# Decoder stack on one core: scores in two rounds of 32 rows, key copies half as wide, row transposes in another bank, two orders changed

## The chip, the cores and the metric

The kernel runs on one core of one Trainium2 chip. The metric is the device time in microseconds (us) of one execution; lower is better.

## The reference

Six attention phases over 32 batches of 64 tokens and width 128, with other work between them. All is float32.

```python
# one phase: q from x; k, v from x (phases 0, 2) or from ctx (1, 3, 4, 5)
Q, K, V = x @ wq + bq, src @ wk + bk, src @ wv + bv      # split into 16 heads of 8, in phase 5 8 heads of 16
A = softmax(where(mask == 0, a large negative, Q K^T / sqrt(dk)))   # phases 0 to 4 have a mask
x = x + (A V) @ wo                                       # then, by phase:
# 0, 1, 4: layer norm; after phase 1 also x = ln(x + relu(x w1 + b1) w2 + b2), then rms norm of it
# 2, 3: the next phase reads rms norm(x); after phase 3: top-2 of 8 experts and a shared one
# 5: x + w2 relu(w1 x + b1) + b2 is the output
```

## The kernel before, in words

A pair is two batches, 128 tokens; a phase has 16 pairs. The work of a pair is cut into stages, and every engine runs a loop over slots: in slot s it does the stage with offset `off` for pair s - off. The offsets are projection 0 (`OFF_PROJ`), values and mask 1 (`OFF_V`), scores 2 (`OFF_SCORE`), transposed probabilities and their product with the values 3 (`OFF_PV`), division by the row sums and output projection 4 (`OFF_OUT`), normalised rows turned to columns 5 (`OFF_XT`), and behind them feed-forward (6 to 9, pairs of phase 1), routing (6 to 9, pairs of phase 3) or the last layers (6 to 8, phase 5). Phases 0 to 3 run as one train of slots, 0 to 72; then come the expert blocks, which the change does not touch; then phases 4 and 5 as a second train. Some slots of a phase are written out, and some come from a hardware loop with addresses in registers. Each engine takes its instructions in the order of `slot`, so a wait holds up all that stands behind it on that engine. Buffers are doubled by the pair's parity.

**Scores.** To multiply all heads at once, GpSimd (POOL) writes `k_by_j`: the keys copied once for each head of a half, each copy with all but one head's rows set to zero by a column of `cst` (L494). TensorE (PE) then runs four products side by side, two halves of 64 rows of queries and keys into two banks, times two batches (L598). With 16 heads a half holds 8 heads, so a copy is 128x1024, and a product has 512 columns. The trace shows eight records, two for each float32 product. VectorE (DVE) takes the maxima `top` (L1140) and the differences `prob` (L1156), ScalarE (ACT) the exponentials (L986); PE transposes them in two halves (L631), ACT copies each half out (L915, L935), and PE multiplies (L759, L770).

**Rows.** The output projection L697 goes to `y`; DVE leaves `spread`, POOL takes the root with `pow` (`rstd` L502, `shift_n` L511), ACT writes `normed` (L922), PE transposes it in bank `B_PROJ` (`XT`, L672), and ACT copies it to `x_t` (L963). The rows of the feed-forward are transposed in bank `B_OUT` (`FB`, L662). Its own root is `rstd_f` (L444, POOL), read by `n_f` (L1118, DVE).

**Order of a slot on PE:** scores; feed-forward out (L616); both transposed halves; routing ranks (L644); values (L656); FB and XT transposes; queries and keys (L687, L688); output projection; feed-forward in (L708); router (L727); mask (L740); products with values (L759), a wait for all that the next scores need (`score_ready`), row sums (L770). **On POOL:** feed-forward, `scaled` and `x_tok` of stage 5, `k_by_j`, root of stage 4, routing. **On ACT:** L915, L922, feed-forward rows, L935, FB copy, queries and keys, XT copy, exponentials, values. **On DVE:** division (L1107, L1110), `n_f` and `y_f` of the feed-forward, `top`, mask, `prob`, routing (`picked` L1178 among it), `y` and its statistics.

## Time and profile before

| what | value |
|---|---|
| runs of the kernel | 704.16, 702.21, 697.53 us; median 702.21 |
| profiled execution | 700.95 us, its span 699.0 us |
| busy | PE 87%, DVE 76%, ACT 68%, POOL 59% |
| chain that ended last | PE 48%, issue 21%, DVE 14%, ACT 8%, POOL 7% |
| mean granted TensorE clock | 0.973 of full speed |

The span is from the first to the last instruction; 1.95 us of the profiled execution lie around it. Busy shares are means over stages with different limits. A timeline row has the start in us from the span's start, the duration, the engine, the line, the operation, what it writes and reads, and in brackets how long the engine was idle before it and what released it.

### The profile page before, as it was taken

What the parts mean: (1) busy time and instruction counts of PE and PEld (TensorE: products, weight loads), DVE (VectorE), ACT (ScalarE), POOL (GpSimd) and SP (SyncE); (2) the same over time, 40 slices, a digit from 0 to 9 for tenths busy, and PEclk for the clock granted to TensorE, in tenths of its full rate; (3) what the DMA queues carried; (4) which work ended last, traced back from release to release, by engine and by line L of the source; (5) the groups of instructions that cost most, each with busy time, mean ns of one, the idle gap of its engine ahead of it and who ended that gap; (6) DMA issues with size and microseconds to landing.
All of it is one profiled execution on the core that took longest, in us unless ns stands there. A gap on an engine that the chain in (4) does not pass through costs nothing.

```text
span 699.0 us, 24529 instructions
## 1 busy us (share of the span) xinstructions
PE 606.7 (87%) x8126; PEld 438.3 (63%) x8126; DVE 529.2 (76%) x1210; ACT 476.9 (68%) x1355; POOL 415.4 (59%) x641
## 2 busy tenths in 40 slices
PE   6888998989998989999767658899996878999996
PEld 3555656666666666666544434799994546666773
DVE  2988899777778899999999852344435788888894
ACT  3677788788878887878655534354533567788994
POOL 5676676778888765565566675055554466665220
PEclk9999999999999999999999978999999899999997
DMA  6433433222444401010111001122225000100110
GB/s 199 122 93 90 105 84 84 53 66 56 107 125 114 126 25 31 26 31 26 32 32 32 25 29 36 35 61 69 66 62 135 17 25 24 30 12 22 36 31 27
DMA packets 49817, 41.97 MB, mean 60 GB/s; under 512 B 6569, under 2 KB 44333, under 8 KB 48704
## 3 DMA queue, kind: packets, MB, share of 16 engines
q1 hardware_dynamic: 41472, 23.13, 11.9%
q10 hardware_dynamic: 5984, 13.45, 8.1%
q0 software_dynamic: 2272, 4.24, 1.8%
q8 instruction: 52, 0.85, 0.5%
q14 instruction: 37, 0.30, 0.1%
HBM read 25.41 MB, written 14.79 MB: 57 GB/s over the span
## 4 chain that ended last, share of the span: by engine, by line
PE 48%; issue 21%; DVE 14%; ACT 8%; POOL 7%; DMA 1%; DVEq 0%; ACTq 0%; POOLq 0%; SPq 0%
PE ps L598 6%; PE ps L824 5%; PE ps L835 5%; PE ps L631 4%; PE ps L759 3%; DVE inv L1107 3%; ACT normed L922 3%; PE ps L687 3%; PE ps L790 3%; PE ps L770 2%; PE ps L708 2%; PE ps L616 2%; DVE prob L1156 2%; PE ps L688 2%; DVE picked L1178 2%
## 5 line engine op out<-in xcount | busy, mean ns | idle before, releaser
L494 POOL TENSOR_TENSOR k_by_j<-k_t,cst 128x1024 f32<-128x1024 f32 (+1 forms) x96 | 168.8, 1758 | 102.8 <-ACT k_t L952 63.0
L1140 DVE TENSOR_REDUCE top<-ps 128x16 f32<-128x1024 f32 (+1 forms) x96 | 108.3, 1128 | 16.6 <-PE ps L598 16.4
L631 PEld LDWEIGHTS ps<-cst,prob 128*128 128x128 f32 x704 | 78.5, 143 | 57.4 <-ACT prob L986 41.1
L986 ACT ACTIVATE prob<-prob 128x1024 f32<-128x1024 f32 (+1 forms) x96 | 95.2, 992 | 20.4 <-DVE prob L1156 19.8
L1156 DVE TENSOR_TENSOR prob<-ps,top 128x1024 f32<-128x1024 f32 (+1 forms) x96 | 108.3, 1128 | 0.7
L1107 DVE RECIPROCAL inv<-ps 128x128 f32<-128x128 f32 x96 | 91.5, 953 | 22.0 <-PE ps L770 21.2
L598 PE MATMUL ps<-k_by_j,q_t 64*64 64x512 f32 (+1 forms) x768 | 102.3, 604 | 0.5 <-POOL k_by_j L494 0.4
L631 PE MATMUL ps<-cst,prob 128*128 128x128 f32 x704 | 98.4, 282 | 1.2 <-ACT prob L986 1.2
L1000 ACT ACTIVATE v<-ps 64x64 f32<-64x64 f32 x320 | 69.0, 216 | 14.2 <-PE ps L770 11.3
L915 ACT ACTIVATE prob_t<-ps 128x512 f32<-128x512 f32 (+1 forms) x96 | 53.8, 560 | 36.2 <-PE ps L631 35.5
L540 POOL DMA_INDIRECT expert_out<-rows_out,rows_in x39 | 38.3, 982 | 53.8 <-DVE rows_out L1309 27.0
L759 PE MATMUL ps<-prob_t,v 128*32 128x64 f32 x2816 | 60.5, 225 | 0.5 <-ACT prob_t L935 0.5
L502 POOL TENSOR_TENSOR rstd<-spread,half_neg 128x1 f32<-128x1 f32 x80 | 44.7, 559 | 24.6 <-DVE spread L1238 22.3
L770 PE MATMUL ps<-prob_t,cst 128*32 128x128 f32 x1408 | 58.2, 278 | 0.8 <-issue 0.8
L759 PEld LDWEIGHTS ps<-prob_t,v 128*32 128x32 f32 x2816 | 44.8, 111 | 20.4 <-issue 18.3
L935 ACT ACTIVATE prob_t<-ps 128x512 f32<-128x512 f32 (+1 forms) x96 | 53.0, 552 | 0.0
L687 PE MATMUL ps<-x_t,wat 128*128 128x128 f32 (+1 forms) x192 | 42.9, 306 | 6.7 <-DMA stage_kv<-in_x_t 5.9
L478 POOL TENSOR_TENSOR scaled<-normed,rows 128x128 f32<-128x128 f32 x48 | 22.0, 459 | 33.4 <-ACT normed L922 33.4
L656 PE MATMUL ps<-wat,stage_kv 128*128 128x128 f32 x192 | 40.3, 292 | 1.7 <-ACT k_t L950 1.3
L824 PE MATMUL ps<-rows_t,first_w 128*128 128x128 f32 x312 | 41.3, 275 | 0.0
L697 PE MATMUL ps<-wat,heads_t 128*128 128x128 f32 x192 | 38.6, 283 | 3.1 <-DVE heads_t L1110 2.7
L835 PE MATMUL ps<-mow,hid_t 128*128 x312 | 41.2, 275 | 0.0
(159 smaller groups left out, 1267.3 us busy)
## 6 DMA issues: line engine op xcount, KB each, us to landing
sorted_rows<-zero_rows ACTq DMA_DIRECT2D x32, 276.2 KB, 2.7
stage_m<-in_m SPq DMA_DIRECT2D x80, 64.0 KB
mow<-in_mow SPq DMA_DIRECT2D x18, 256.0 KB, 3.0
stage_kv<-in_ctx_t SPq DMA_DIRECT2D x64, 64.0 KB
rows_in<-sorted_rows SPq DMA_DIRECT2D x39, 65.0 KB
x_t<-in_x_t SPq DMA_DIRECT2D x16, 64.0 KB, 1.9
stage_kv<-in_x_t SPq DMA_DIRECT2D x16, 64.0 KB
stage_kv<-x_t SPq DMA_DIRECT2D x16, 64.0 KB
```

Of the source, the lines that this page charges most:

```text
L494: pool.tensor_tensor(k_by_j[:, p, 0:nj, :], k_t[:, p:p + 1, :].broadcast_to([128, nj, TOK]), cst[:, cj:cj + nj].unsqueeze(2).broadcast_to( ...
L598: mm = pe.matmul(ps[S * b:S * b + S, 2 * p + bank, 0:nj * S].rearrange("p (h k) -> p h k", k=S), q_t[rows_h, p, S * b:S * b + S], k_by_j[r ...
L631: mm = pe.transpose(ps[:, 2 * p + half, k * 128:(k + 1) * 128], prob[:, p, q * 128:(q + 1) * 128], ident)
L759: mm = pe.matmul(ps[32 * g:32 * g + 32, B_HEADS, S * b:S * b + S], vb[:, p, b, q, :], prob_t[:, p, half, c * 128 + S * b:c * 128 + S * b + S],
L770: mm = pe.matmul(ps[32 * g:32 * g + 32, B_HEADS, 128:128 + TOK], own_ones(pr, k), prob_t[:, p, half, c * 128:c * 128 + TOK], start=k == 0, ...
L824: mm = pe.matmul(ps[:, B_H[j % 2], c * 128:(c + 1) * 128], first_w[:, j % 2, c * 128:(c + 1) * 128], rows_t[:, j % 2, :], start=True, stop ...
L835: mm = pe.matmul(ps[:, B_Y[j % 2], 0:D], hid_t[:, j % 2, c * 128:(c + 1) * 128], mow2[:, bass.ds(e, 1), c * 128:(c + 1) * 128].rearrange(" ...
L986: act.activation(prob[:, p, 0:w], prob[:, p, 0:w], ACT.Exp, scale=float(D // heads(pr)) ** -0.5).then_inc(exp_d, 1)
L1000: ins = act.activation(dst, src[:, :, par, :].rearrange("r (g k) d -> r g k d", k=2), ACT.Copy)
L1107: dve.reciprocal(inv[:, p, :], ps[:, B_HEADS, 128:128 + TOK]).then_inc(inv_d, 1)
L1140: dve.tensor_reduce(top[:, p, 0:nh].rearrange("p (b h) -> p b h", b=2), sc, AX.X, ALU.max).then_inc(top_d, 1)
L1156: dve.tensor_tensor(prob[:, p, 0:nh * S].rearrange("p (b h k) -> p b h k", b=2, k=S), sc, top[:, p, 0:nh].rearrange("p (b h) -> p b h", b= ...
```

## The change

1. `k_by_j` has one copy for each head of a group of 32 rows: four copies (two with 8 heads) in place of eight (four). The scores are made in two rounds: round 0 takes groups 0 and 2, round 1 groups 1 and 3, each round four products of half as many columns as before. Round 1 stands between the two transposed halves of the pair ahead, and waits for round 0 through `round_d`.
2. XT and FB transposes are written to free columns of bank `B_HEADS` and stand behind the query and key projections. They wait for `heads_d`; the products with values, which write that bank, wait for the copies `xt_e` and `f_xt`.
3. The wait `score_ready` in the midst of the products with values goes; its waits stand ahead of round 0.
4. On ACT L922 stands ahead of L915, and the FB copy behind the query and key copies. On POOL the root of stage 4 stands ahead of `k_by_j`.

```diff
         q_t, k_t = sb("q_t", [128, 2, TOK]), sb("k_t", [128, 2, TOK])
-        k_by_j = sb("k_by_j", [128, 2, 8, TOK])
+        k_by_j = sb("k_by_j", [128, 2, 4, TOK])
...
         B_PROJ, B_HEADS, B_OUT, B_F = 4, 5, 6, 7
-        FB, OUT, XT = (slice(128 * n, 128 * n + 128) for n in range(1, 4))
+        OUT, XT, FB = (slice(128 * n, 128 * n + 128) for n in range(1, 4))
...
 
-                pr = at(OFF_PROJ)
-                if pr is not None:
-                    p, nj = pr.p, heads(pr) // 2
-                    cj = C_J16 if nj == 8 else C_J8
-                    wait_pair(pool, k_e, pr)
-                    wait_pair(pool, score_d, pr, 2)
-                    pool.tensor_tensor(k_by_j[:, p, 0:nj, :], k_t[:, p:p + 1, :].broadcast_to([128, nj, TOK]),
-                                       cst[:, cj:cj + nj].unsqueeze(2).broadcast_to([128, nj, TOK]), ALU.mult)\
-                        .then_inc(kj_d, 1)
                 pr = at(OFF_OUT)
                 if pr is not None and POST[pr.phase] != "none":
                     p = pr.p
@@ -511,6 +503,15 @@
                         pool.tensor_tensor(shift_n[:, p, :], minus[:, p, :], rstd[:, p, :], ALU.mult).then_inc(shift_d, 1)
                     else:
                         pool.sem_inc(shift_d, 1)
+                pr = at(OFF_PROJ)
+                if pr is not None:
+                    p, nj = pr.p, heads(pr) // 4
+                    cj = C_J16 if nj == 4 else C_J8
+                    wait_pair(pool, k_e, pr)
+                    wait_pair(pool, score_d, pr, 2)
+                    pool.tensor_tensor(k_by_j[:, p, 0:nj, :], k_t[:, p:p + 1, :].broadcast_to([128, nj, TOK]),
+                                       cst[:, cj:cj + nj].unsqueeze(2).broadcast_to([128, nj, TOK]), ALU.mult)\
+                        .then_inc(kj_d, 1)
...
-
-            def score(pr):
-
-                p, nj = pr.p, heads(pr) // 2
+            def score_round(pr, r):
+
+                if r == 1:
+                    wait_pair(pe, round_d, pr)
+                p, nj = pr.p, heads(pr) // 4
                 masked = MASKED[pr.phase]
                 for bank in range(2):
-                    rows_h = slice(S * bank, S * bank + S)
+                    rows_g = slice(32 * (2 * bank + r), 32 * (2 * bank + r) + 32)
                     for b in range(2):
                         mm = pe.matmul(
-                            ps[S * b:S * b + S, 2 * p + bank, 0:nj * S].rearrange("p (h k) -> p h k", k=S),
-                            q_t[rows_h, p, S * b:S * b + S], k_by_j[rows_h, p, 0:nj, S * b:S * b + S],
-                            start=not masked, stop=True, skip_group_check=True)
-                mm.then_inc(score_d, 1)
+                            ps[S * b:S * b + S, 2 * p + bank, r * nj * S:(r + 1) * nj * S].rearrange("p (h k) -> p h k", k=S),
+                            q_t[rows_g, p, S * b:S * b + S], k_by_j[rows_g, p, 0:nj, S * b:S * b + S],
+                            start=not masked and r == 0, stop=True, skip_group_check=True)
+                return mm
...
                 pr = at(OFF_SCORE)
                 if pr is not None:
-                    if isinstance(pr.n, int):
-                        score_ready(pr)
-                    score(pr)
+                    p = pr.p
+                    wait_pair(pe, pt1_e, pr, 2)
+                    if MASKED[pr.phase]:
+                        wait_pair(pe, mask_d, pr)
+                    wait_pair(pe, q_e, pr)
+                    wait_pair(pe, kj_d, pr)
+                    score_round(pr, 0).then_inc(round_d, 1)
...
@@ -631,6 +630,9 @@
                             mm = pe.transpose(ps[:, 2 * p + half, k * 128:(k + 1) * 128],
                                               prob[:, p, q * 128:(q + 1) * 128], ident)
                         mm.then_inc(done, 1)
+                        scored = at(OFF_SCORE)
+                        if half == 0 and scored is not None:
+                            score_round(scored, 1).then_inc(score_d, 1)
...
                     wait_pair(pe, v_e, pr, 1)
-                    turned = at(OFF_XT + 1)
-                    if turned is not None:
-                        wait_pair(pe, xt_e, turned)
                     mm = pe.matmul(ps[:, B_PROJ, 256:384], stage_kv[:, p, :], wat[:, ph, 2, :], start=True, stop=True)
                     mm.then_inc(vproj_d, 1)
...
-                    pe.transpose(ps[:, B_OUT, FB], xn_f[:, done.p, :], ident).then_inc(f_back, 1)
-                pr = at(OFF_XT)
-                if pr is not None:
-                    wait_pair(pe, norm_d, pr)
-                    projected = at(OFF_PROJ + 1)
-                    if projected is not None:
-                        wait_pair(pe, k_e, projected)
-                    valued = at(OFF_V + 1)
-                    if valued is not None:
-                        wait_pair(pe, v_e, valued)
-                    pe.transpose(ps[:, B_PROJ, XT], row_buffer(pr), ident).then_inc(xt_d, 1)
...
                         .then_inc(proj_d, 1)
+                pr = at(OFF_SCORE)
+                if pr is not None and at(OFF_PV) is None:
+                    score_round(pr, 1).then_inc(score_d, 1)
+
+                divided = at(OFF_OUT)
+                pr = follows(at, OFF_FB, FF)
+                if pr is not None:
+                    if divided is not None:
+                        wait_pair(pe, heads_d, divided)
+                    wait_own(pe, f_xn, pr)
+                    pe.transpose(ps[:, B_HEADS, FB], xn_f[:, pr.p, :], ident).then_inc(f_back, 1)
+                pr = at(OFF_XT)
+                if pr is not None:
+                    if divided is not None:
+                        wait_pair(pe, heads_d, divided)
+                    wait_pair(pe, norm_d, pr)
+                    pe.transpose(ps[:, B_HEADS, XT], row_buffer(pr), ident).then_inc(xt_d, 1)
+
                 pr = at(OFF_OUT)
                 if pr is not None:
...
                     wait_pair(pe, heads_d, pr)
-                    before = follows(at, OFF_FB, FF)
-                    if before is not None:
-                        wait_own(pe, f_xt, before)
-
...
                     wait_pair(pe, v_e, pr)
                     wait_pair(pe, heads_d, pr, 1)
+                    turned = at(OFF_XT)
+                    if turned is not None:
+                        wait_pair(pe, xt_e, turned)
+                    turned = follows(at, OFF_FB, FF)
+                    if turned is not None:
+                        wait_own(pe, f_xt, turned)
                     wait_pair(pe, pt0_e, pr)
...
 
-                    following = at(OFF_V)
-                    if following is not None:
-                        score_ready(following)
...
                         .then_inc(l_o, 1)
-                pr = at(OFF_PV)
-                if pr is not None:
-                    p = pr.p
-                    w = 128 * (heads(pr) // 4)
-                    wait_pair(act, pv_d, pr, 2)
-                    wait_pair(act, pt0_d, pr)
-                    act.activation(prob_t[:, p, 0, 0:w], ps[:, 2 * p, 0:w], ACT.Copy).then_inc(pt0_e, 1)
                 pr = at(OFF_XT)
                 if pr is not None and POST[pr.phase] == "ln":
                     p = pr.p
@@ -921,6 +915,13 @@
                     wait_pair(act, res_d, pr, 2)
                     act.activation(normed[:, p, :], y[:, p, :], ACT.Identity, bias=shift_n[:, p, :], scale=rstd[:, p, :])\
                         .then_inc(norm_d, 1)
+                pr = at(OFF_PV)
+                if pr is not None:
+                    p = pr.p
+                    w = 128 * (heads(pr) // 4)
+                    wait_pair(act, pv_d, pr, 2)
+                    wait_pair(act, pt0_d, pr)
+                    act.activation(prob_t[:, p, 0, 0:w], ps[:, 2 * p, 0:w], ACT.Copy).then_inc(pt0_e, 1)
...
 
-                pr = follows(at, OFF_FB, FF)
-                if pr is not None:
-                    wait_own(act, f_back, pr)
-                    act.activation(x_t[:, bass.ds(pr.i * TOK, TOK)], ps[:, B_OUT, FB], ACT.Copy, scale=v("n1"))\
-                        .then_inc(f_xt, 1)
...
                             act.activation(dst[:, p, :], src, ACT.Copy).then_inc(done, 1)
+
+                pr = follows(at, OFF_FB, FF)
+                if pr is not None:
+                    wait_own(act, f_back, pr)
+                    turned = at(OFF_XT)
+                    if turned is not None:
+                        wait_pair(act, xt_d, turned)
+                    act.activation(x_t[:, bass.ds(pr.i * TOK, TOK)], ps[:, B_HEADS, FB], ACT.Copy, scale=v("n1"))\
+                        .then_inc(f_xt, 1)
                 pr = at(OFF_XT)
                 if pr is not None:
                     ph = pr.phase
                     wait_pair(act, xt_d, pr)
-                    dst, src = x_t[:, bass.ds(pr.i * TOK, TOK)], ps[:, B_PROJ, XT]
+                    dst, src = x_t[:, bass.ds(pr.i * TOK, TOK)], ps[:, B_HEADS, XT]
```

The columns of `cst` are made to fit: `C_J16` is `r % 32 // 8 == arange(4)`, and `C_J8` is `r % 32 // 16 == arange(2)`.

## Rows read from the trace of the kernel before

**Rows 1.** Timeline of PE, phase 1: start, us, engine, line, op [idle before]
```profile
108.19 1.09 PE L598 MATMUL ps<-k_by_j,q_t 64*64 64x512 f32 x8
...
109.21 1.09 PE L631 MATMUL ps<-cst,prob 128*128 128x128 f32 x8
...
110.14 0.39 PE L656 MATMUL ps<-wat,stage_kv 128*128 128x128 f32 x2
...
110.99 0.33 PE L672 MATMUL ps<-cst,normed 128*128 128x128 f32 x1 [0.47 <-ACT normed L922]
...
111.16 0.40 PE L687 MATMUL ps<-x_t,wat 128*128 128x128 f32 x2
...
111.39 0.39 PE L688 MATMUL ps<-stage_kv,wat 128*128 128x128 f32 x2
...
112.27 0.65 PE L759 MATMUL ps<-prob_t,v 128*32 128x64 f32 x32
...
113.29 1.09 PE L598 MATMUL ps<-k_by_j,q_t 64*64 64x512 f32 x8
```

**Rows 2.** Timeline of ACT in the same slot
```profile
111.81 0.37 ACT L950 ACTIVATE q_t<-ps,vec 128x128 f32<-128x128 f32 x1 [0.39 <-PE ps L688]
...
112.33 0.46 ACT L963 ACTIVATE x_t<-ps,vec 128x128 f32<-128x128 f32 x1
```

**Rows 3.** Timeline of PE, phase 0, first slots
```profile
37.77 0.33 PE L672 MATMUL ps<-cst,normed 128*128 128x128 f32 x1 [1.46 <-ACT normed L922]
```

**Rows 4.** Timeline of DVE and ACT, phase 2 without feed-forward
```profile
286.10 1.21 DVE L1140 TENSOR_REDUCE top<-ps 128x16 f32<-128x1024 f32 x1
...
287.37 1.22 DVE L1156 TENSOR_TENSOR prob<-ps,top 128x1024 f32<-128x1024 f32 x1
...
288.62 1.06 ACT L986 ACTIVATE prob<-prob 128x1024 f32<-128x1024 f32 x1 [0.75 <-DVE prob L1156]
```

**Rows 5.** Timeline of POOL, DVE and PE, slot with feed-forward
```profile
206.71 0.55 POOL L502 TENSOR_TENSOR rstd<-spread,half_neg 128x1 f32<-128x1 f32 x1
...
207.63 0.55 POOL L444 TENSOR_TENSOR rstd_f<-spread_f,half_neg 128x1 f32<-128x1 f32 x1
...
208.23 0.34 DVE L1118 TENSOR_SCALAR n_f<-y_f,mom_f,rstd_f 128x128 f32<-128x128 f32 x1
...
209.03 0.29 DVE L1126 TENSOR_TENSOR y_f<-ps,x_tok 128x128 f32<-128x128 f32 x1 [0.47 <-PE ps L616]
...
210.85 0.33 PE L662 MATMUL ps<-cst,xn_f 128*128 128x128 f32 x1 [0.76 <-ACT xn_f L929]
...
213.60 0.15 DVE L1235 TENSOR_SCALAR spread<-moments 128x1 f32<-128x1 f32 x1
```

**Rows 6.** Line L1107, one per slot: count, ns least/median/most, first and last start
```profile
L1107 DVE RECIPROCAL inv<-ps x6: 956/957/959, 199.4 to 236.8; 128x128 f32<-128x128 f32 x6
...
L1107 DVE RECIPROCAL inv<-ps x12: 945/947/948, 265.1 to 318.4; 128x128 f32<-128x128 f32 x12
...
L1107 DVE RECIPROCAL inv<-ps x11: 947/952/957, 318.4 to 390.3; 128x128 f32<-128x128 f32 x11
```

**Rows 7.** Timeline of DVE and POOL in one routing slot
```profile
370.62 2.54 DVE L1178 TENSOR_TENSOR picked<-hot,rank 128x16 f32<-128x16 f32 x1
...
371.21 1.90 POOL L494 TENSOR_TENSOR k_by_j<-k_t,cst 128x1024 f32<-128x1024 f32 x1
```

**Rows 8.** Source lines of DVE without a PSUM operand, whole kernel: count, ns least/median/most
```profile
L1178 DVE TENSOR_TENSOR picked<-hot,rank x16: 157/166/2544, 334.2 to 427.5; 128x16 f32<-128x16 f32 x16
...
L1238 DVE CUSTOM_DVE_ANT_0 squares<-y x32: 291/824/1729, 228.1 to 411.3; 128x128 f32<-128x128 f32 x32
...
L1320 DVE TENSOR_TENSOR x_tok<-mow,x_tok x8: 415/762/1681, 530.4 to 567.9; 128x256 f32<-128x256 f32 x8
```

**Rows 9.** Timeline of POOL and PE in phase 5, eight heads
```profile
667.08 1.04 POOL L494 TENSOR_TENSOR k_by_j<-k_t,cst 128x512 f32<-128x512 f32 x1 [2.70 <-ACT k_t L952]
...
667.32 0.66 PE L598 MATMUL ps<-k_by_j,q_t 64*64 64x256 f32 x8
```

More of the change, by code:

```diff
@@ L70 @@
 BIASED = {0: 0, 1: 1, 4: 2}
-C_ID, C_J16, C_J8, C_IOTA, C_BASE = 0, 128, 136, 140, 148
-C_STEP, C_UPTO, C_BLOCK = 156, 172, 236
+C_ID, C_J16, C_J8, C_IOTA, C_BASE = 0, 128, 132, 134, 142
+C_STEP, C_UPTO, C_BLOCK = 150, 166, 230
 C_O16 = C_BLOCK + JB
@@ L266, in build @@
         neg_d, mask_d = sem("neg_d"), sem("mask_d")
+        round_d = sem("round_d")
         minus_d, shift_d = sem("minus_d"), sem("shift_d")
@@ L581, in _ @@
             pe.wait_ge(loaded["wat"], 16)
-            def score_ready(pr):
-                wait_pair(pe, pt1_e, pr, 2)
-                if MASKED[pr.phase]:
-                    wait_pair(pe, mask_d, pr)
-                wait_pair(pe, q_e, pr)
-                wait_pair(pe, kj_d, pr)
-            def score(pr):
-                p, nj = pr.p, heads(pr) // 2
+            def score_round(pr, r):
+                if r == 1:
+                    wait_pair(pe, round_d, pr)
+                p, nj = pr.p, heads(pr) // 4
                 masked = MASKED[pr.phase]
                 for bank in range(2):
-                    rows_h = slice(S * bank, S * bank + S)
+                    rows_g = slice(32 * (2 * bank + r), 32 * (2 * bank + r) + 32)
                     for b in range(2):
                         mm = pe.matmul(
-                            ps[S * b:S * b + S, 2 * p + bank, 0:nj * S].rearrange("p (h k) -> p h k", k=S),
-                            q_t[rows_h, p, S * b:S * b + S], k_by_j[rows_h, p, 0:nj, S * b:S * b + S],
-                            start=not masked, stop=True, skip_group_check=True)
-                mm.then_inc(score_d, 1)
+                            ps[S * b:S * b + S, 2 * p + bank, r * nj * S:(r + 1) * nj * S].rearrange("p (h k) -> p h k", k=S),
+                            q_t[rows_g, p, S * b:S * b + S], k_by_j[rows_g, p, 0:nj, S * b:S * b + S],
+                            start=not masked and r == 0, stop=True, skip_group_check=True)
+                return mm
             def slot(at):
@@ L652, in slot @@
                     wait_pair(pe, v_e, pr, 1)
-                    turned = at(OFF_XT + 1)
-                    if turned is not None:
-                        wait_pair(pe, xt_e, turned)
                     mm = pe.matmul(ps[:, B_PROJ, 256:384], stage_kv[:, p, :], wat[:, ph, 2, :], start=True, stop=True)
                     mm.then_inc(vproj_d, 1)
-                done = follows(at, OFF_FB, FF)
-                if done is not None:
-                    wait_own(pe, f_xn, done)
-                    pe.transpose(ps[:, B_OUT, FB], xn_f[:, done.p, :], ident).then_inc(f_back, 1)
-                pr = at(OFF_XT)
-                if pr is not None:
-                    wait_pair(pe, norm_d, pr)
-                    projected = at(OFF_PROJ + 1)
-                    if projected is not None:
-                        wait_pair(pe, k_e, projected)
-                    valued = at(OFF_V + 1)
-                    if valued is not None:
-                        wait_pair(pe, v_e, valued)
-                    pe.transpose(ps[:, B_PROJ, XT], row_buffer(pr), ident).then_inc(xt_d, 1)
                 pr = at(OFF_PROJ)
@@ L1349, in constants @@
     cst[:, C_ID:C_ID + 128] = np.eye(128)
-    cst[:, C_J16:C_J16 + 8] = r[:, None] % S // 8 == np.arange(8)
-    cst[:, C_J8:C_J8 + 4] = r[:, None] % S // 16 == np.arange(4)
+    cst[:, C_J16:C_J16 + 4] = r[:, None] % 32 // 8 == np.arange(4)
+    cst[:, C_J8:C_J8 + 2] = r[:, None] % 32 // 16 == np.arange(2)
     cst[:, C_IOTA:C_IOTA + E] = np.arange(E)
```

## Prediction

> **What bounds the kernel now.** I read the page's shares first (in the table above): PE is busy 87% and DVE 76%, and no engine is full on average. So I went through the timeline stage by stage and asked in each which loop from one slot to the next has no slack. There are four kinds of slot.
>
> *Layer-norm slots without other work* (phases 0, 1 and 4, some 30 of them). PE goes from scores to scores in 5.10 us and stands 0.47 ahead of the XT transpose for `normed` [rows 1]. The loop is XT, queries and keys, their copy on ACT, the `k_by_j` copy of 1.90 on POOL (the length is that of [rows 7]), the root queued behind it, `normed`, XT again [rows 1, 2]. In the first slots of phase 0 that wait is 1.46 [rows 3].
>
> *Feed-forward slots* (14 full ones). The period is (236.8 - 199.4) / 5 = 7.5 [rows 6], PE waits 0.76 for `xn_f` [rows 5], and DVE is in step with POOL: `n_f` starts 0.05 after `rstd_f` ends, at 208.18 [rows 5].
>
> *Routing slots.* Ten periods take 390.3 - 318.4 = 71.9 us [rows 6]. `picked`, 16 elements in a row, takes 0.16 at least and 0.17 in the median, but here 2.54: it ends at 373.16, when the `k_by_j` copy of POOL ends (373.11) [rows 7, 8]. Where all of DVE's operands lie in SBUF, it waits for a copy of POOL to end. `squares` takes 0.29 at least and 0.82 in the median for this reason, and the combination of expert rows (L1320) 0.42 at least and 1.68 at most [rows 8]. The Trainium skill says the same in "SBUF — State Buffer", in the section on the shared pair: it is an exclusive lock for the whole instruction, taken by a DVE operation with two SBUF inputs or a GpSimd operation, and the loser blocks. The trace agrees (2.54 against 0.16).
>
> *Phase 5* has copies of 1.04 and scores of 0.66 [rows 9], and PE without idle time.
>
> **The change, part by part.**
>
> *Rounds.* The score records span 1.09 with 512 columns and 0.66 with 256 [rows 1, 9], so 256 columns are worth 0.43. The step from scores to the next instruction is 109.21 - 108.19 = 1.02; with 256 columns it is 0.59, and 0.16 of each is fixed. Two rounds cost 1.18, 0.16 more for each slot with 16 heads, and the same for 8 heads. A group of 32 rows is not in the trace. Below, a round can cost nothing fixed, 0.43; above, two of the four products of a round might not overlap, and it takes 1.02 like the whole set of before. I take 0.59, the nearest row. The maxima now wait for round 1 and so for half of the transposes: 0.59 + 0.465 + 0.66 = 1.72 after the start of the scores, where it was 1.09 (half of the transposes is (110.14 - 109.21) / 2 = 0.465) [rows 1].
> That rounds interleaved with full transposes change the array's tiling twice more per slot is what the Trainium skill warns of in "TensorEngine Tiling (Array Packing)", Key Properties: a change of tiling mode drains TensorE. By the rule each entry costs something; the fixed 0.16 of a set of four may be this drain.
>
> *Narrow copies.* A 128x512 copy took 1.04 [rows 9] against 1.90: 0.86 less of POOL for each of 80 slots. In phase 5 it is 128x256 and not in the trace; by the same step it is 1.04 - 0.43 = 0.6, at best 0.52, at worst 1.04.
>
> *The root ahead of the copy, `normed` first.* The loop through the copy is broken in the layer-norm slots. What is late next? PE's own order, with the new wait for `xt_e` ahead of the products with values. The key projection starts at 0.59 + 0.465 + 0.59 + 0.465 + 0.23 + 0.23 = 2.57 after the scores (steps of 0.23 between projections, 111.39 - 111.16 [rows 1]). From there ACT's copy of the queries starts 0.42 later, the XT copy 0.52 after that, and it lasts 0.46 [rows 1, 2]: 3.97. The products start at 4.0 and the next scores 113.29 - 112.27 = 1.02 later: 5.02 to 5.05. Before, the products followed 0.88 after the key projection [rows 1]; now it is 1.43, so about 0.4 of PE's old wait comes back at the new place. Behind that wait are queued the products, the row sums and the next scores, and DVE's division waits for them. A second loop comes with round 1, since it stands behind transposes that wait for the exponentials: 0.465 + 0.66 for transposes and round 1, 1.27 from maxima to differences, 1.25 to the exponentials, 1.06 for them [rows 4], and two hand-overs of 0.05: 4.8. So a layer-norm slot takes 5.05 for 5.10, with up to 0.2 more where the hardware loop ran slower: -2 over 30 slots (-5 to +2).
> *Plain slots of phase 2.* DVE loses its block at `squares`, but the period before is (318.4 - 265.1) / 11 = 4.85 [rows 6], and the new loop of 4.8 takes over: 0 (-3 to +3).
> *Start.* The wait of 1.46 in the first slots goes down to the steady one, and the first scores wait for a copy that is 0.86 shorter: -3 (0 to -4).
>
> *Feed-forward slots.* Here the new order on POOL closes a loop. The copy now stands behind the root of stage 4, which waits for `spread`, and ahead of `rstd_f`, for which DVE stands at `n_f`. From the end of `spread`: 0.1 to the root, 207.63 - 206.71 = 0.92 to the end of `shift_n`, 1.0 for the copy [rows 9], 0.55 for `rstd_f`, 0.05 to `n_f`; `n_f` 0.34; and 213.75 - 209.03 = 4.72 from `y_f` to the end of `spread` [rows 5]. The sum is 7.7, and the period before is 7.5. The earlier feed-forward transposes and the gone wait of 0.76 on PE bring nothing then: 0 over 14 slots. Bounds: if a few of DVE's steps shorten with POOL less busy, or PE alone sets it (7.5 - 0.76 + 0.16 = 6.9), -8; if the loop costs its full sum, +3.
>
> *Routing slots.* The copy now runs behind the root, while DVE divides and takes maxima out of PSUM, and 4 us ahead of `picked`. The period of full slots, about 7.8 (with two short slots of 5.5 the other eight make up 71.9 with 7.6 on average), loses 2.54 - 0.16 = 2.38 and gets the later maxima (1.72 - 1.09 = 0.63): 6.05. Two slots at 5.0 and eight at 6.05 are 58.4, so -13.5. `chosen` waits behind the copy, 1.0 later after the root, but PE reaches the ranks then only. What can keep part of the block: POOL's indirect transfers and its two copies of rows can still meet `picked`. The gain has 5 and 13.5 as bounds; I take 10.
>
> *Restart of phase 4.* Four of the combinations took 1.1 to 1.7 where 0.42 is enough, 4.3 in sum (least and most of eight are in the row) [rows 8]. They run just behind `spread`, now ahead of the copy. First copy -0.9; the transposes and the second round ahead of the maxima give back 0.6 in four slots: -3 (0 to -5).
>
> *Phase 5.* PE is full, and gets 0.16 for the second round and part of the new wait, since ACT's copies need 1.1 to 1.4 after the keys: +0.2 in 16 slots, +3 (0 to +6). No block on DVE's last sum is worth anything while PE is the bound.
>
> *No cost:* the moved `score_ready` (its waits are long over by the next slot, as the copy is made two slots ahead), the bank change itself (`heads_d` is awaited by the output projection right behind).
>
> Sum: -3 - 2 + 0 + 0 - 10 - 3 + 3 = -15. Against the profiled 700.95 this is 686; the median of the runs lies 1.3 above it, and I predict 687.5 beside a median of 702.2.
>
> **The rivals.**
>
> *A. Rounds that do not overlap (slower).* If a round of 32 rows takes not 0.59 but 0.59 + d, then some 30 layer-norm, 13 plain, 8 routing and 16 slots of phase 5 get 2d, or d by the second loop: about 65 x 2d = 130d. It eats the 15 from d = 0.12. With d = 0.2, half way to products that run by twos, it is +26: 713. For it: no product of 32 rows is in the trace, and each entry into another tiling drains. Against: four products of 64 rows overlap, and 32 products on tiles of 32 columns start within 0.47. The drain rule of the page, with the fixed 0.16 twice per round in place of once, is d = 0.16: 708.
>
> *B. The block moves instead of going (same).* POOL's row copies and transfers come back to back, and `picked` waits for their end; the copy meets `n_f` and the mask row instead. Routing then gives 4, the restart 1.5, and feed-forward slots lose 0.1 each: 698. For it: POOL is busy 59% of the span. Against: the median of `picked` is 0.17 with those transfers running.
>
> *C. Feed-forward slots go with PE (faster still).* If `n_f` does not bind, 14 slots go to 6.9 at best: -8, and 679. Against: the sum of 7.7 above, for which every step is in the rows.
>
> **How the numbers follow.** Forecast 55%, C 15%, B 17%, A 13%. The half widths of the terms together (root of the sum of squares of 5, 5, 3, 3, 3, 2) are about 9 either way; the range from 677 to 704 holds the forecast, C and B, and leaves most of A and the ends out. A difference of under 1% (7 us) is about what a measurement of this kernel can tell from none. Faster by more than that, under 695.2: forecast and C, some of B: 0.72. Within 1%: most of B, the edges of forecast and A: 0.17. Slower: A: 0.11.
>
> **What would show it.** `k_by_j` at 1.04 in 80 slots. Score records 0.6 to 0.7 in span, two sets per slot; a longer set is A. `picked` at 0.2 and L1107 at 6.0 to 6.5 apart between 340 and 390; if it stays at 7, B. In layer-norm slots PE idle ahead of L759 with ACT's XT copy (L963) as releaser, and none ahead of L672. In feed-forward slots `n_f` waiting on `rstd_f`, and the period still 7.4 to 7.7; at 7.0, C. Phase 5 at 3.8 or more. The prediction is wrong above all if one loop that I found closed has slack, since 14 or 30 slots hang on each.

## The result and the profile after

The changed kernel takes 705.25 us (median of 16 runs, 702.43 to 708.17) beside 702.17 for the kernel before on the same chip (697.53 to 704.76, 16 runs): a ratio of 1.0055, interval 1.0034 to 1.0076. The forecast was 687.5. The profiled execution took 707.85 with a span of 706.0, 7.0 more than before. The page's first part of the changed kernel (busy us, share, instructions):

```profile
PE 617.7 (87%) x8894; PEld 455.4 (64%) x8894; DVE 496.1 (70%) x1210; ACT 496.3 (70%) x1355; POOL 337.4 (48%) x641
```

POOL is busy 78 us less and DVE 33 less, and the kernel is not faster: the work that went was not what the slots wait for.

`inv` (L1111 now) runs once per slot, so its starts divide the span. The table is worked out from these starts; "changed again" is a second profile of the changed kernel, "before again" one of the kernel before. The last column is the prediction's term.

```
stage (slots)          before  before again  changed  changed again  difference  predicted
start (4)               40.4      37.1        42.6       43.1          +2.2       -3
phase 0 (9)             47.4      47.5        48.9       48.9          +1.4 }
phase 1 (6)             30.7      30.7        32.1       32.1          +1.4 }     -2
phase 4, full (10)      51.7      51.7        53.6       53.6          +2.0 }
feed-forward (20)      141.5     141.6       138.4      138.4          -3.2        0
plain (12)              58.4      58.4        61.4       61.4          +3.0        0
routing (10)            71.9      71.5        61.1       61.0         -10.8      -10
drain and experts      157.5     156.3       165.6      159.3          +8.0      none
restart (4)             27.9      27.9        25.8       26.4          -2.1       -3
phase 5 (17)            60.9      61.0        66.1       66.1          +5.2       +3
```

The difference column compares the first profiles. In the slots from phase 0 to routing, and in phases 4 and 5, two profiles of one program agree within 0.4 us. The start and the experts do not repeat: the experts took 137.8 to 145.9 us over all the profiles of this study, and changed and changed again differ by 6.3 in drain and experts. The view by windows shows a part of why. The first fence is of the changed kernel, the second of the same kernel profiled again (columns: window, PE busy with its instructions, granted clock, DMA share, GB/s), each from the last slot of the drain on.

```profile
404.70:424.70 20.00, 13.13 (x38) 0.62 0.10 31
...
444.70:464.70 20.00, 20.00 (x171) 0.94 0.20 53
```

```profile
402.40:422.40 20.00, 12.84 (x45) 0.74 0.10 31
...
442.40:462.40 20.00, 19.94 (x179) 1.00 0.22 58
```

PE, busy only 13 of 20 us there, was granted 0.62 instead of 0.74 of its clock, and 0.94 for 1.00 in the next but one window; the experts alone are 3.6 us longer there. So most of the +8.0 belongs to that execution. Without drain and experts the differences sum to -0.9; with those of changed again (+1.8) to +0.9, and the medians say +3.1. The 2 us between are of the size by which start and experts differ between executions, and were not resolved further. The forecast had -15 in the place of the -0.9, so its terms are off by 14 in sum.

The layer-norm slot that answers to [rows 1], PE and then ACT in the timeline of the changed kernel:

```profile
107.33 0.66 PE L593 MATMUL ps<-k_by_j,q_t 32*64 32x256 f32 x8
107.92 0.66 PE L630 MATMUL ps<-cst,prob 128*128 128x128 f32 x4
108.51 0.66 PE L593 MATMUL ps<-k_by_j,q_t 32*64 32x256 f32 x8
109.10 0.66 PE L630 MATMUL ps<-cst,prob 128*128 128x128 f32 x4
109.59 0.39 PE L655 MATMUL ps<-wat,stage_kv 128*128 128x128 f32 x2
...
110.04 0.39 PE L672 MATMUL ps<-stage_kv,wat 128*128 128x128 f32 x2
110.26 0.27 PE L690 MATMUL ps<-cst,normed 128*128 128x128 f32 x1
...
111.65 0.65 PE L763 MATMUL ps<-prob_t,v 128*32 128x64 f32 x32 [0.55 <-issue]
...
112.67 0.66 PE L593 MATMUL ps<-k_by_j,q_t 32*64 32x256 f32 x8
```

```profile
110.47 0.37 ACT L946 ACTIVATE q_t<-ps,vec 128x128 f32<-128x128 f32 x1
...
110.98 0.46 ACT L968 ACTIVATE x_t<-ps,vec 128x128 f32<-128x128 f32 x1
```

Three things are to be seen. The round of 32 rows takes what was forecast (span 0.66, step 0.59). The wait at XT is gone: L690 follows L672 without idle time, where it was 0.47 [rows 1]. And the whole of it is back, 0.55 long, ahead of the products with values (L763), which start 0.21 after ACT's XT copy ends (110.98 + 0.46 = 111.44). The profile names "issue" as releaser and not ACT. But in nearly every layer-norm slot, plain slot and slot of phase 5 the products start 0.20 to 0.21 after that copy ends, with idle times ahead of them of mostly 0.54 to 0.62, 0.27 to 0.35 and 0.30 to 0.38; and the profile of run 2 names the copy. The chain that ended last holds, in this stretch of the changed kernel, nothing but PE and this piece (start, length, what):

```profile
110.76 0.34 PE ps L738 x4
111.10 0.55 issue
111.65 0.65 PE ps L763 x32
112.30 0.44 PE ps L771 x16
```

The source lines that answer to [rows 8] and [rows 6] (count, ns least/median/most, first and last start; the first `inv` row is eleven periods of full feed-forward slots, the second the plain slots, the third the routing slots):

```profile
L1182 DVE TENSOR_TENSOR picked<-hot,rank x16: 157/164/247, 338.4 to 424.8; 128x16 f32<-128x16 f32 x16
...
L1242 DVE CUSTOM_DVE_ANT_0 squares<-y x32: 291/292/293, 231.9 to 408.6; 128x128 f32<-128x128 f32 x32
...
L1324 DVE TENSOR_TENSOR x_tok<-mow,x_tok x8: 409/424/425, 527.3 to 568.9; 128x256 f32<-128x256 f32 x8
...
L1111 DVE RECIPROCAL inv<-ps x12: 956/957/958, 157.9 to 238.9; 128x128 f32<-128x128 f32 x12
...
L1111 DVE RECIPROCAL inv<-ps x13: 956/957/958, 261.9 to 323.3; 128x128 f32<-128x128 f32 x13
...
L1111 DVE RECIPROCAL inv<-ps x11: 950/952/958, 323.3 to 384.4; 128x128 f32<-128x128 f32 x11
```

Every block of DVE is gone: `picked` at most 0.25 (2.54 before), `squares` 0.29 throughout, the combination 0.43 at most. Routing slots are 6.11 apart on average; the full ones are 6.3 apart (7.8 before), where 6.05 was forecast. Plain slots are (323.3 - 261.9) / 12 = 5.12 apart, where 4.86 was to stay.

A feed-forward slot, DVE and POOL in the timeline of the changed kernel, answering to [rows 5]:

```profile
210.30 0.15 DVE L1239 TENSOR_SCALAR spread<-moments 128x1 f32<-128x1 f32 x1
...
213.03 0.35 DVE L1122 TENSOR_SCALAR n_f<-y_f,mom_f,rstd_f 128x128 f32<-128x128 f32 x1 [1.30 <-POOL rstd_f L445]
```

```profile
211.45 1.04 POOL L512 TENSOR_TENSOR k_by_j<-k_t,cst 128x512 f32<-128x512 f32 x1
212.45 0.55 POOL L445 TENSOR_TENSOR rstd_f<-spread_f,half_neg 128x1 f32<-128x1 f32 x1
```

DVE stands 1.30 for `rstd_f` behind root and copy, as forecast; the period is (238.9 - 157.9) / 11 = 7.36 (7.56 over the same eleven slots before, 7.7 as the sum had it).

### The profile page after: what moved, and what is told of

Its sections match the earlier page's. It is cut to its first block, busy times and chain, and to the rows that moved or that the text cites. A ratio compares the mean times of both kernels' runs of the same rounds, so it can differ in the third digit from the quotient of the medians.

```text
span 706.0 us, 25942 instructions
## 1 busy us (share of the span) xinstructions
PE 617.7 (87%) x8894; PEld 455.4 (64%) x8894; DVE 496.1 (70%) x1210; ACT 496.3 (70%) x1355; POOL 337.4 (48%) x641
## 4 chain that ended last, share of the span: by engine, by line
PE 64%; issue 17%; DVE 8%; POOL 6%; ACT 2%; DMA 1%; DVEq 0%; POOLq 0%; SPq 0%; ACTq 0%
PE ps L593 12%; PE ps L630 10%; PE ps L763 6%; PE ps L825 5%; PE ps L836 5%; PE ps L771 4%; PE ps L738 3%; PE ps L791 3%; PE ps L671 2%; PE ps L655 2%; PE ps L672 2%; PE ps L695 2%; PE ps L801 2%; DVE prob L1160 2%; POOL rstd_f L445 1%
## 5 line engine op out<-in xcount | busy, mean ns | idle before, releaser
L593 PE MATMUL ps<-k_by_j,q_t 32*64 32x256 f32 (+1 forms) x1536 | 124.3, 393 | 1.2 <-issue 0.3
L512 POOL TENSOR_TENSOR k_by_j<-k_t,cst 128x512 f32<-128x512 f32 (+1 forms) x96 | 93.1, 970 | 66.6 <-ACT k_t L948 37.4
L630 PE MATMUL ps<-cst,prob 128*128 128x128 f32 x704 | 119.5, 290 | 2.3 <-ACT prob L990 2.1
L630 PEld LDWEIGHTS ps<-cst,prob 128*128 128x128 f32 x704 | 76.5, 143 | 62.1 <-issue 47.1
L1111 DVE RECIPROCAL inv<-ps 128x128 f32<-128x128 f32 x96 | 91.8, 956 | 22.8 <-PE ps L771 20.0
L763 PE MATMUL ps<-prob_t,v 128*32 128x64 f32 x2816 | 60.5, 225 | 30.5 <-issue 27.7
L763 PEld LDWEIGHTS ps<-prob_t,v 128*32 128x32 f32 x2816 | 46.7, 111 | 53.1 <-issue 53.1
L936 ACT ACTIVATE prob_t<-ps 128x512 f32<-128x512 f32 (+1 forms) x96 | 53.6, 558 | 19.0 <-PE ps L630 18.3
L593 PEld LDWEIGHTS ps<-k_by_j,q_t 32*64 32x64 f32 x1536 | 40.8, 133 | 38.0 <-issue 37.4
L541 POOL DMA_INDIRECT expert_out<-rows_out,rows_in x39 | 38.3, 983 | 53.3 <-DVE rows_out L1313 29.3
L771 PE MATMUL ps<-prob_t,cst 128*32 128x128 f32 x1408 | 60.0, 277 | 0.0
L671 PE MATMUL ps<-x_t,wat 128*128 128x128 f32 (+1 forms) x192 | 39.5, 289 | 7.8 <-DMA stage_kv<-in_x_t 7.3
L825 PE MATMUL ps<-rows_t,first_w 128*128 128x128 f32 x312 | 42.9, 282 | 0.0
L825 PEld LDWEIGHTS ps<-rows_t,first_w 128*128 128x128 f32 x312 | 39.4, 198 | 0.0
```

Of the source, the lines that this page charges most:

```text
L512: pool.tensor_tensor(k_by_j[:, p, 0:nj, :], k_t[:, p:p + 1, :].broadcast_to([128, nj, TOK]), cst[:, cj:cj + nj].unsqueeze(2).broadcast_to( ...
L593: mm = pe.matmul(ps[S * b:S * b + S, 2 * p + bank, r * nj * S:(r + 1) * nj * S].rearrange("p (h k) -> p h k", k=S), q_t[rows_g, p, S * b:S ...
L630: mm = pe.transpose(ps[:, 2 * p + half, k * 128:(k + 1) * 128], prob[:, p, q * 128:(q + 1) * 128], ident)
L763: mm = pe.matmul(ps[32 * g:32 * g + 32, B_HEADS, S * b:S * b + S], vb[:, p, b, q, :], prob_t[:, p, half, c * 128 + S * b:c * 128 + S * b + S],
L771: mm = pe.matmul(ps[32 * g:32 * g + 32, B_HEADS, 128:128 + TOK], own_ones(pr, k), prob_t[:, p, half, c * 128:c * 128 + TOK], start=k == 0, ...
L825: mm = pe.matmul(ps[:, B_H[j % 2], c * 128:(c + 1) * 128], first_w[:, j % 2, c * 128:(c + 1) * 128], rows_t[:, j % 2, :], start=True, stop ...
```

## The experiments

The suspects are the two rounds, the new XT place with its wait ahead of the products, the order on POOL, and the start. In the edits only the core stands. Runs 1 to 4, 5 to 8, and 9 and 10 shared a chip each; the kernel before had medians of 699.04, 699.43 and 701.11 there. All ratios are to the kernel before on the same chip; runs of different groups are compared by their ratios. Runs 3, 5 and 6 have four executions each, 8 and 9 one, the others ten. A run's stage times come from one profiled execution, which can lie some us off the median. Feed-forward periods are over the eleven slots of the first section.

**1. The rounds alone.**

```
 before.py: score(pr)  ->  score_round(pr, 0) ... score_round(pr, 1), k_by_j 4 copies wide;
 POOL, ACT and the transposes as in the kernel before
```

> The kernel before with the two rounds and the narrow copies alone; transposes, orders of ACT and POOL and the early wait for the scores stay as before. Theory W (the changed kernel loses its gain to the new wait of the products with values for the XT copy): without that wait layer-norm slots are set by PE's own work at about 4.9, plain slots of phase 2 at 4.9, phase 5 at 3.8; the routing slots keep a block of a narrow copy, 7.8 - 0.9 = 6.9; feed-forward slots 7.2. Sum about 688. Rival R (the rounds themselves cost more than the narrow copies give, 0.3 per slot for four changes of tiling): 96 slots by 0.3 less the narrow copies' 10, about 720; layer-norm slots stay at 5.3.

Measured: 692.84, ratio 0.9911 (0.9874 to 0.9947). Plain slots 4.94 apart, routing 6.59, phases 0, 1 and 4 128.2 in all (129.7 before, 134.6 changed), phase 5 60.6. The rounds with narrow copies don't lose in the layer-norm slots or in phase 5; in the plain slots they lose 1.0 in all. Their largest gain lies in the feed-forward stage, 134.4 for 141.5 before, where the changed kernel has 138.4, and so has run 3, which differs from this one in little but the orders on POOL and ACT. In routing `picked` still runs into the copy, for the shorter time that it has now:

```profile
L1187 DVE TENSOR_TENSOR picked<-hot,rank x16: 159/171/1682, 326.7 to 414.7; 128x16 f32<-128x16 f32 x16
```

**2. The change without rounds**, one set of 64 rows with copies of 1.90.

```
 after.py: score_round(pr, 0/1)  ->  score(pr), k_by_j 8 copies wide,
 score_ready(following) between the products as before
```

> The changed kernel with the scores in one set of 64 rows and the wide copies again (the wait for the next scores stands in the midst of the products as before); transposes in the bank of heads and both new orders stay. Theory W: layer-norm slots still wait for the XT copy: key projection at 2.4, then 1.6 and 1.0: 5.0. Feed-forward slots get 0.9 longer through the wide copy ahead of rstd_f, 8.2; routing slots 7.0; phase 5 3.7. Sum about 705. Rival R: slots shrink by the full cost of the rounds, sum under 695.

Measured: 696.73, ratio 0.9952 (0.9932 to 0.9971). Phase 4 is 50.7 (53.6 changed), plain slots 4.79, phase 5 63.0 (66.1 changed), but feed-forward slots went from 7.36 to 8.20: the copy of 1.90 in the loop of root, copy and `rstd_f`. The sum of 705 was missed by 8, above all since routing slots did not go to 7.0: they take 62.1 in all with the wide copy too (61.1 changed, 71.9 before), and `picked` is 0.25 at most. Here the profile names ACT's XT copy ahead of the products with values, in the slot that answers to [rows 1]:

```profile
113.76 0.65 PE L759 MATMUL ps<-prob_t,v 128*32 128x64 f32 x32 [0.52 <-ACT x_t L967]
```

**3. XT and feed-forward transposes back** in their old banks and places, all else as changed.

```
 after.py, PE: transpose(ps[:, B_HEADS, XT]) behind the projections
   -> transpose(ps[:, B_PROJ, XT]) ahead of them;
 no wait for xt_e ahead of the products with values
```

> The changed kernel with the XT and FB transposes in their old banks and places, with their old waits; rounds, narrow copies, and both new orders stay. Theory W: PE has no wait ahead of the products, and none at XT since normed comes first: layer-norm slots 4.9 (now 5.34), plain 4.85 (now 5.1), phase 5 3.75 (now 4.0), feed-forward slots unchanged at 7.35 (set by rstd_f behind the copy), routing unchanged at 6.3. Sum about 688. Rival R: layer-norm slots stay above 5.2 and the time within 1% of the changed kernel.

Measured: 692.29, ratio 0.9888 (0.9856 to 0.9919). Phases 0, 1 and 4 take 127.8 (5.0 to 5.2 for a slot, not 4.9), phase 5 60.4, plain slots 4.94, routing unchanged at 61.0. In nine of the plain slots PE stands at the first transposes for the exponentials, the second loop of the prediction:

```profile
272.75 0.66 PE L630 MATMUL ps<-cst,prob 128*128 128x128 f32 x4 [0.16 <-ACT prob L988]
```

So the new transposes, with the wait that comes with them, cost 1.7% or 12 us (the stages from phase 0 to phase 5 without drain and experts give 14), and the order on POOL is worth its routing gain without them.

**4. The copy ahead of the root again.**

```
 after.py, POOL: k_by_j ahead of rstd, minus, shift_n instead of behind them
```

> The changed kernel with the key copy ahead of the root on POOL again, all else as changed. Theory P (in feed-forward slots DVE waits at n_f for rstd_f behind the copy; in routing slots the late copy is what frees picked): feed-forward slots go to 7.0 from 7.35, routing slots to 6.9 from 6.3, layer-norm slots unchanged at 5.34 since their bound is the XT copy. Sum 704 to 706. Rival: the order on POOL is worth what it was meant for in the layer-norm slots, and these lengthen to over 5.5: 712.

Measured: 701.88, ratio 1.0036 (1.0011 to 1.0061). Feed-forward slots fell from 7.36 to 6.68, routing slots rose from 6.11 to 6.55 (`picked` at most 1.68 again); phases 0, 1 and 4 stayed at 134.7. Root or copy first is indifferent to the layer-norm slots as long as XT's copy bounds them, and the two other kinds give -10.6 (feed-forward, the shorter slots at both ends included) and +4.4. The profiles bear this out (spans 699.2 and 706.0, drain and experts 166 in both), the ratios show only 1.3 of it. Part of that is which execution was profiled: the changed kernel's lies 2.6 above its median, this one's 0.9 below. The rest is open.

**5. Copies deferred in feed-forward slots** (on top of 3): there POOL makes the copy one slot later, behind `rrms_f`.

```
+    pr = at(OFF_V)        # behind rrms_f
+    if pr is not None and follows(at, OFF_FN, FF) is not None: k_by_j copy
-    if pr is not None:    # behind shift_n
+    if pr is not None and follows(at, OFF_FN - 1, FF) is None: k_by_j copy
```

> The kernel with the transposes back in their old banks and places (692.3 us, 0.989 of before), and the key copy of feed-forward slots made in the next slot, behind rstd_f and rrms_f; elsewhere it stays behind the root. If n_f behind the copy is what sets the 11 full feed-forward slots (7.44 there, 6.68 with the copy first), they go to 6.7, the ramps before and behind with them: -9 in the span, routing unchanged at 6.1. About 683. Rival: something else holds these slots, and only the copy ahead of the root frees them: 7.4 and no change.

Measured: 686.84, ratio 0.9853 (0.9803 to 0.9903), an interval that overlaps that of run 3. Feed-forward slots 7.17 (7.44 in run 3, 6.7 expected), `n_f` without a wait; routing stays 60.8. The wait was there and went, but half of the gain did not come: PE is now without a marked idle time, and from the values to the output projection it takes 1.20 with the transposes in their old place, where the kernel of run 4 takes 0.89. So in these slots the new place looks the better one; no run changes it alone.

**6. The same with one set of 64 rows and wide copies.**

```
 run 5: score_round(pr, 0/1)  ->  score(pr), k_by_j 8 copies wide
```

> The last kernel, but with the scores in one set of 64 rows and the wide copies, as before the change. Theory: two rounds are a loss wherever PE's order is the bound, and their narrow copies buy nothing once the copy stands behind the root and out of the way of rstd_f. Layer-norm slots 4.7 (DVE's own work) for 5.0 to 5.2, plain slots 4.8, feed-forward slots 6.6 to 6.8, routing 6.3, phase 5 3.4 to 3.5: 672 to 678. Rival: the wide copy of 1.9 is missed somewhere else, in routing slots (7.0) or in feed-forward slots (7.5): 690.

Measured: 676.96, ratio 0.9684 (0.9630 to 0.9738), the fastest of all, 22 us under the kernel before. Of the change it keeps the root ahead of the copy and `normed` first on ACT, and it has the deferred copies of run 5; the wait `score_ready` is back too. The plain slots, and `picked`, in the source lines of this kernel:

```profile
L1117 DVE RECIPROCAL inv<-ps x13: 956/958/959, 254.8 to 308.3; 128x128 f32<-128x128 f32 x13
```

```profile
L1188 DVE TENSOR_TENSOR picked<-hot,rank x16: 158/165/254, 322.6 to 407.2; 128x16 f32<-128x16 f32 x16
```

Plain slots are (308.3 - 254.8) / 12 = 4.46 against 4.94 in run 5, and the restart 23.4 against 26.9; routing gives 2.0 back (62.9) and the feed-forward stage 3.1 (136.7 for 133.7, where 6.6 to 6.8 for a slot was expected and 7.2 measured). Phases 4 and 5 are unchanged to 0.1, so there the rounds cost nothing; 4.7 and 3.4 were expected and 5.05 and 3.55 measured. The total fell in the range by other terms than those forecast. With the copies off the path, the rounds are a net cost of 10 us by the medians (686.84 against 676.96, four executions each) and of 7 by the profiled spans (681.8 and 674.6): 5.8 in plain slots, 3.5 in the restart and 1.7 in the start, less what feed-forward and routing give back; 2.2 more lie in drain and experts.

**7. The changed kernel with ACT's XT copy ahead of the copies of queries and keys.**

```
 after.py, ACT: x_t<-ps (XT) ahead of q_t, k_t <- ps
```

> The changed kernel with one order changed on ACT: the XT copy ahead of the copies of queries and keys. Theory W: the products wait for this copy, which ends 1.40 after the key projection starts; alone in front it ends about 0.9 to 1.0 after, so layer-norm slots go from 5.34 to 4.9, plain ones from 5.12 to 4.9, phase 5 from 3.8 to 3.5, feed-forward unchanged at 7.36. About 693. Rival R (the rounds on PE set these slots): no change from 705.

Measured: 695.9, ratio 0.9947 (0.9918 to 0.9976). Moving one copy of 0.46 by two places on ACT gives back 1.1%. The idle time ahead of the products fell from 0.55 to 0.23 in the timeline of this kernel, and phase 4 to 50.6, the value without the new transposes:

```profile
113.14 0.65 PE L763 MATMUL ps<-prob_t,v 128*32 128x64 f32 x32 [0.23 <-issue]
```

So the wait for XT's copy is what run 3 took away. Plain slots are 4.99. Phase 5 keeps over half of its loss (63.9, or 3.8 for a slot, where 3.5 was expected).

**8. The changed kernel again**, one execution.

> The changed kernel once more, for a second profile. If the 5.5 us that the expert blocks took more in its first profile come from the clock of TensorE in that one execution, they move; if they belong to the kernel, 145 stays, where before had 140.

Measured: 702.17, span 700.4. All slot stages repeated, drain and experts came 6.3 shorter (first section).

**9. The kernel before again**, one execution.

> The kernel before once more, one look, for the spread between two profiles of one program. The drain behind routing took 17.8 us, the experts 139.8 and the first score round's stage 24.5 in its first profile; TensorE's granted clock in the drain differed between executions of the changed kernel (20.3 and 17.6 us). If that is the program's, this profile repeats 139.8 and 17.8 within 0.3; if it is chance, the experts come anywhere from 139.8 to 142 here, and the loops of the other stages repeat within 0.3%.

Measured: 696.33, span 694.4. The experts repeated (140.0), the drain came 1.4 shorter, and the start 3.3 shorter; the other stages repeated within 0.1 but for routing, 0.4 shorter. In the start PE's records have two lengths: in its first profile the 128x128 pair of the key projection took 0.63 until 14 us and 0.39 from 20 on, here 0.39 from 12.6 on, after an idle time of 0.74. These are lengths as of the two levels of the clock, 1.2 and 2.4 GHz, though the granted clock reads 1.00 throughout. When PE comes to the higher level differs between executions, and the start that is 3.3 shorter goes with it.

**10. Round 1 at once in the slots without products.**

```
 after.py, PE:  score_round(pr, 0)
+               if at(OFF_PV) is None: score_round(pr, 1)    # was behind the projections
```

> The changed kernel, but in the slots that have no products with values yet round 1 of the scores stands right behind round 0, not behind the values and the projections of the next pair. Theory (the start loses its 2.7 us because round 1 of the first pair, ready at 10.5, waits for projections whose input lands at 13.9, until 14.6): the first maxima start at 11.2 to 11.7 us of the span rather than 15.8, the stage up to the second reciprocal takes 24.5 to 25 us for 27.3, the restart of phase 4 perhaps 1 less than 25.8, and all else stays: 702 to 703 beside 705.2. Rival (the load of the third pair sets the start in any case): maxima early, stage still 27, time unchanged.

Measured: 701.17, ratio 1.0012 (0.9974 to 1.0049), against 1.0055 for the changed kernel: 3 us less, though the intervals overlap. The profiled execution, 694.99, is the fastest of the ten and 6 under their median, so its stage times flatter the kernel. The first maxima on DVE, in this kernel and then in the changed one:

```profile
11.62 1.22 DVE L1143 TENSOR_REDUCE top<-ps 128x16 f32<-128x1024 f32 x1 [5.18 <-PE ps L593]
```

```profile
15.76 1.22 DVE L1144 TENSOR_REDUCE top<-ps 128x16 f32<-128x1024 f32 x1 [9.62 <-PE ps L593]
```

The stage to the first `inv` is 22.7 for 27.3. Part of that is again PE's records reaching 0.39 earlier (from 18.6 us, beyond 23.4 in the changed kernel). That this goes with the placement shows over all profiles: in the seven of kernels that hold round 1 back, the first projection at the short length comes at 23.9 to 29.3 us, in the five others (both of the kernel before, runs 2, 6 and 10) at 11.2 to 19.7. No run separates it from the later maxima. The restart stayed at 26.3, so the placement of round 1 is not what holds it at 26 to 27.

## Why the prediction was wrong

*Bounds and blocks: right.* DVE's blocks, the loop of root, copy and `rstd_f`, and PE's wait for XT were where they were said to be. Routing gave 10.8 for 10, the restart 2.1 for 3; the narrow copies take 1.04, and 0.61 in phase 5 for the 0.6 worked out. That routing came out so close is in part luck: the sum gave 13.5, the 10 was chosen under it, and full slots are 6.3 and not 6.05. It is mostly the order on POOL that gives it: with the root first and the wide copy, routing takes 62.1 (run 2) and 62.9 (run 6), 9 to 10 under before, while the narrow copies alone give 6 (run 1). The rule of the Trainium skill cited for this, in "SBUF — State Buffer", holds with numbers: a `picked` of 0.16 takes 2.54, 1.68 and 0.16 to 0.25 as the copy it meets is wide, narrow or elsewhere.

*Rounds: the score step right, what follows it mis-sized.* The step "half of the transposes is 0.465" failed. The first four take 0.59 and the others 0.49, so scores and transposes take 0.59 + 0.59 + 0.59 + 0.49 = 2.26 for 1.95 before: 0.31 more and not 0.16. The price stands on the transposes next to the rounds. The drain rule of the Trainium skill ("TensorEngine Tiling (Array Packing)", Key Properties) gives no size: rival A took it for 0.32 per slot over the forecast, and 0.15 was measured. That the 0.15 is a drain is not shown; the rows agree with one. In phase 5 and in the layer-norm slots the rounds cost nothing by themselves (runs 1, 3 and 6); in the plain slots they do.

*The XT loop: the step that cost the forecast.* "The products start at 4.0" was to be 0.03 behind ACT's XT copy and 1.43 behind the key projection, which was to start at 2.57. Measured: 2.71 + 0.43 + 0.51 + 0.46 + 0.21 + 1.02 = 5.34. The difference of 0.32 from 5.02 is 0.14 from the transposes and 0.18 from the hand-over to the products, for which I had taken 0.03 to 0.05. So the term that failed is this loop's sum, 5.05 for a slot that takes 5.35 to 5.43 on average in each phase: +4.8 over the 25 slots of the table instead of -2. Runs 3 and 7 show the cause from two sides: without the wait 5.04 in phase 4, with ACT's copy two places earlier 5.06. The loss also needs the rounds: without them a slot of phase 4 falls to 5.07 (run 2), where the key projection starts 0.31 earlier and the wait for the copy is still there.

*Plain slots: the same loop left out.* I set them by the loop of the exponentials, 4.8, though XT and its wait are there too. It reads 287.49 to 292.55 = 5.06 in one slot; 5.12 on average. Even the forecast's own 5.02 for the XT loop would have given +2 here. The loop of the exponentials was itself close: without the XT wait it binds, with PE's wait of 0.16 for them (run 3), and the slots are 4.94, which fits 4.8 and the 0.13 that the first transposes take longer. Without the rounds they are 4.46 (run 6): with the XT wait and the copy both off the path, this is where the rounds cost.

*Phase 5: sign right, size 5.2 for 3.* Without the XT wait none of it is left (60.4 to 60.6, runs 1 and 3), so the 0.16 for the second round was not due by itself. With the wait the rounds are over half of it: without them phase 5 takes 63.0 (run 2), 2.1 over before.

*Feed-forward slots: -3.2 for 0.* The loop was the right one, at 7.36 and not 7.7: the 4.72 from `y_f` to the end of `spread` is 4.49 to 4.50 now (from 205.95 to 210.45). Rival C was wrong for this kernel and right for the order of run 4 (6.68, under the 6.9 that I took for PE's bound). So the new order on POOL, priced at 0 here, costs 10.6 beside the order of run 4, more than it gives in routing (4.4).

*Start: +2.2 for -3.* What the copy saved, round 1 lost: in the slots without products it stands behind projections that wait for a load, and the first maxima came 4.6 later than before (15.76 against 11.19). This placement was in the diff and I did not cost it. The size is uncertain, as one program's start varies by 3; run 10 gives 3 back in the whole, with intervals that overlap.

*Drain and experts* were no term. They came 8.0 longer in the profiled execution. Kernels that share this part with the changed one took from 157.1 (run 10) to 166.1 (run 4), beside 157.5 and 156.3 before, so the runs leave open how much of it is the change's.

The terms against what they came to: layer-norm slots +6.8 over the forecast, the start +5.2, plain slots +3, phase 5 +2.2, restart +0.9, and to the other side feed-forward -3.2 and routing -0.8. They sum to the 14 of the first section, and 12 of it lie in the slots with the XT wait.

The rivals: A's loss came in half its size and elsewhere; B did not occur (and its own terms sum to 696, not 698). What decided was none of the three: a wait that I had found and priced at 0.4 of PE's old idle time gave back more than all of it.

## What to carry to other kernels

When a wait is moved rather than removed, work out the new loop through every engine's queue with measured hand-overs, and apply it in every kind of slot that contains it; here one loop, missed by 0.3 us in 25 slots, left out in 12 and priced too low in 17, came to 12 us, most of what the forecast had promised. Look for the order on the third engine before giving up a change: ACT's copy two places earlier gave back 1.1%. A narrow operation is worth its extra rounds only where the wide one is on the path; once it was moved off the path (run 6), the wide one was the better by 7 to 10 us. And a new order that frees one kind of slot can bind another: the root ahead of the copy gives 4.4 in routing and costs 10.6 in the feed-forward stage (run 4).

## What the runs showed of the hardware

- Products on tiles of 32 rows by 64 columns overlap in fours: 256 columns each span 0.66, as with 64 rows. Full transposes next to such rounds take longer, 0.59 for four between two rounds and 0.49 for the last four, where eight in a row took 0.93.
- From the end of an ACT copy to the first of 32 small products that wait for it 0.21 passes, and 0.05 from the end of `rstd_f` on POOL to the start of `n_f` on DVE [rows 5]. The idle time ahead of the products is mostly named "issue" in the profile.
- PE's records in the first 11 to 24 us have lengths as of 1.2 GHz at a granted clock that reads 1.00. The end of that stretch differs between executions of one program, and it comes later in the kernels that hold round 1 of the first pairs back.
